# Transposed scores a tick later, head tiles loaded four ticks ahead, a second buffer for the MLP's hidden units, and eight slots of second-layer weights

## The reference

```python
def _L0_xattn_ref(tgt, memory, Wq, Wk, Wv):
    ...
    probs = jax.nn.softmax(scores, axis=-1)
    ...
    tgt2 = att[0]
    return tgt + tgt2

def _L1_xattn_ref(x, y, ...):
    ...
    attn = jax.nn.softmax(jnp.einsum('bhmd,bhnd->bhmn', q, k) * SCALE, axis=-1)
    ...
    x = x + o @ Wproj + bproj
    h = layer_norm(x, gm, bm)
    h = jax.nn.gelu(h @ W1 + b1, approximate=False)
    x = x + h @ W2 + b2
    return x
```

## Time and profile before

| | before |
|---|---|
| runs, us | 1812.53, 1810.10, 1816.04; median 1812.53 |
| profiled execution, us | 1814.68, span 1812.9 |
| VectorE, ScalarE, GpSimd busy, us | 1083.6, 1154.6, 938.3 |
| a matmul of 512 columns, ns (pipelined; start to start about 230) | 395 to 404 |
| an exponential of 128 x 512, ns | 600 |
| VectorE's subtraction for a low half, ns | 690 |
| GpSimd's subtraction for a low half, ns | 1290 |
| mean granted clock of TensorE | 0.987 |

### The profile page before, as it was taken

One profiled execution on the slowest core, in us unless ns is written; L12 is line 12 of the kernel. 1 busy time (PEld: TensorE's weight loads), 2 busy tenths in 40 slices (PEclk: granted clock), 3 DMA queues, 4 the chain that ended last, 5 costly groups with the idle time before them and its releaser, 6 DMA issues.

```text
span 1812.9 us, 23964 instructions
## 1 busy us (share of the span) xinstructions
PE 1724.4 (95%) x7488; PEld 1323.2 (73%) x7488; DVE 1083.6 (60%) x1860; ACT 1154.6 (64%) x1935; POOL 938.3 (52%) x802
## 2 busy tenths in 40 slices
PE   6899998998989899999999999999999999999898
PEld 5677776766666677777777777777777777777686
DVE  4566665477777566666665665666666656563322
ACT  3677764587877665766765576667657665874231
POOL 0454556157665464655555554646555545555241
PEclk8999999999999999999999999999999999999999
DMA  6688989675545575686666566756756675677262
GB/s 233 210 297 282 306 281 362 225 223 173 169 129 185 154 201 135 183 234 163 169 199 187 143 161 187 203 139 194 230 154 165 200 189 147 166 211 242 98 205 93
DMA packets 157102, 354.69 MB, mean 196 GB/s; under 512 B 29232, under 2 KB 47792, under 8 KB 156080
## 3 DMA queue, kind: packets, MB, share of 16 engines
q1 hardware_dynamic: 106096, 187.21, 35.5%
q10 hardware_dynamic: 50880, 165.95, 29.3%
HBM read 251.51 MB, written 82.08 MB: 184 GB/s over the span
## 4 chain that ended last, share of the span: by engine, by line
PE 69%; ACT 9%; issue 5%; DMA 5%; DVE 5%; POOL 4%; SPq 2%; ACTq 1%; DVEq 0%; POOLq 0%
PE ps_d L863 46%; PE ps_o L884 11%; PE ps_t L917 6%; PE ps_s L902 5%; DMA q_st<-negmax_t 2%; ACT p_hi L1026 1%; DMA rs<-o_raw 1%; ACT ps_t L1033 1%; ACT ps_d L937 1%; POOL p_lo L1288 1%; ACT ht L998 1%; PE ps_d L793 1%; DVE negmax L1176 1%; SPq L713 1%; DVE stats L1133 1%
## 5 line engine op out<-in xcount | busy, mean ns | idle before, releaser
L1288 POOL TENSOR_TENSOR p_lo<-p_full,p_hi 128x512 fp32r<-128x512 f32 x288 | 371.4, 1290 | 593.3 <-ACT p_full L1033 592.9
L1026 ACT ACTIVATE p_hi<-ps_t 128x512 fp32r<-128x512 f32 x576 | 345.3, 600 | 364.4 <-PE ps_t L917 359.6
L1176 DVE TENSOR_REDUCE negmax<-ps_s 128x1 fp32r<-128x512 f32 x576 | 389.2, 680 | 135.3 <-PE ps_s L902 134.9
L863 PE MATMUL ps_d<-hT,w_r 128*128 128x512 f32 x1536 | 422.1, 395 | 1.4 <-DVE hT L1081 1.3
L863 PE MATMUL ps_d<-w_r,g_s 128*128 128x512 f32 x1536 | 391.3, 394 | 5.5 <-DMA w_r<-w_scratch 5.5
L863 PEld LDWEIGHTS ps_d<-hT,w_r 128*128 128x128 f32 x1536 | 290.1, 190 | 74.0 <-DVE hT L1081 5.4
L863 PEld LDWEIGHTS ps_d<-w_r,g_s 128*128 128x128 f32 x1536 | 290.6, 190 | 71.2 <-issue 7.1
L1189 DVE TENSOR_TENSOR p_lo<-ps_t,p_hi 128x512 fp32r<-128x512 f32 x288 | 198.8, 690 | 232.2 <-ACT ps_t L1033 231.3
L917 PE MATMUL ps_t<-q_st,k_st 97*128 97x512 f32 x576 | 232.9, 404 | 17.3 <-DMA q_st<-negmax_t 12.1
L884 PE MATMUL ps_o<-p_hi,v_s 128*65 128x512 f32 x576 | 232.3, 403 | 12.6 <-POOL p_lo L1288 6.4
L902 PE MATMUL ps_s<-k_st,q_st 96*128 96x512 f32 x576 | 232.1, 403 | 5.3 <-DVE negmax L1176 5.0
(11 more groups left out here) (99 smaller groups left out, 2174.5 us busy)
## 6 DMA issues: line engine op xcount, KB each, us to landing
w_r<-w_scratch ACTq DMA_DIRECT2D x214, 512.0 KB, 4.9
w_r<-w_scratch SPq DMA_DIRECT2D x42, 512.0 KB, 4.7
v_scratch<-v_out SPq DMA_DIRECT2D x36, 520.0 KB, 5.1
k_scratch<-kq_out SPq DMA_DIRECT2D x36, 512.0 KB, 5.2
q_st<-q_scratch SPq DMA_DIRECT2D x144, 128.0 KB, 4.4
k_st<-k_scratch SPq DMA_DIRECT2D x144, 128.0 KB, 4.2
o_ab<-o_raw SPq DMA_DIRECT2D x144, 128.0 KB, 3.8
w_scratch<-piece_out SPq DMA_DIRECT2D x16, 1024.0 KB, 6.2
```

Of the source, the lines that this page charges most:

```text
L863: ins = nc.tensor.matmul(bank(u), lhs[a], rhs[b], start=(i == 0 and m == 0), stop=(i == 3 and m == 2))
L1026: act.activation(p_hi[:, c], ps_t[:, c % 2], ACT.Exp, scale=SCALE)
L1176: dve.tensor_reduce(negmax[:, h % 2, c:c + 1], ps_s[:, c % 2], AX.X, ALU.max, negate=True).then_inc(s_maxed, 1)
L1288: pool.tensor_tensor(p_lo[:, c], p_full[:, (by_gpsimd(s) - 1) % 2], p_hi[:, c].bitcast(F32), ALU.subtract).then_inc(p_pool_split, 1)
```

## The change

SHIFT goes from 7 to 8 and WEIGH from 9 to 10, STACK_AHEAD from 5 to 4. `h_st` becomes two buffers that lie in the low halves of the two slots of `g_s`: hidden units are emptied there, GELU is applied there in place, and GpSimd overwrites them with the low half. VectorE's wait for the low halves is removed; that a slot is free follows from the order of TensorE's units. The room goes to the second layer's ring, which has eight slots. In the first MLP block (n = 1, ticks of block 2) the turns and the first four hidden units are spread over 13 ticks instead of 9, the first burst is four ticks later, and two hidden units of the next group stand in front of its tick, where there was nothing.

```diff
--- before.py
+++ after.py
@@ -45,10 +45,10 @@
 
 
 
-SHIFT = 7
-WEIGH = 9
+SHIFT = 8
+WEIGH = 10
 POOL_CHUNKS = (0, 2)
-STACK_AHEAD = 5
+STACK_AHEAD = 4
 PRE = 6
 
 COST = {"a": 2.0, "tg": 2.0, "ht": 2.0}
@@ -204,9 +204,9 @@
             else:
                 spread(range(at + 15, at + 22), outs)
                 spread(range(at + 22, at + 35), queries[-6:])
-                spread(range(at + 35, at + 44), turns + hidden(new, 0))
-                burst(at + 44, new, 0, [])
-                spread(range(at + 45, at + 55), hidden(new, 1))
+                spread(range(at + 35, at + 48), turns + hidden(new, 0))
+                burst(at + 48, new, 0, hidden(new, 1)[:2])
+                spread(range(at + 49, at + 55), hidden(new, 1)[2:])
             burst(at + 55, new, 1, second(new, 0)[:2])
             spread(range(at + 56, at + CH + 5), second(new, 0)[2:] + hidden(new, 2))
 
@@ -375,7 +375,7 @@
 
 
 
-W1_RING, W2_RING = 4, 6
+W1_RING, W2_RING = 4, 8
 W1_PIECES = [(n, c) for n in range(1, NP) for c in range(HC)]
 
 
@@ -484,7 +484,7 @@
     g_at = place[0]
     g_s = sb("g_s", [P, 2, 2, 4, T], F32R)
     h_at = place[0]
-    h_st = sb("h_st", [P, 4, T], F32)
+    h_st = [sb(f"h_st_{i}", [P, 4, T], F32, at=g_at + 4 * (2 * i + 1) * 4 * T) for i in range(2)]
     w2_at = place[0]
     w2_r = sb("w2_r", [P, W2_RING, 2, D], F32R)
     w1_at = place[0]
@@ -610,6 +610,9 @@
         if i < PIECES // 2:
             return w1_raw[:, i % 2].rearrange("p c (k j) -> p c k j", k=FC)
         return w2_raw[:, i % 2]
+
+    def hidden_of(n, group):
+        return h_st[GELU_NO[n, group] % 2][:]
 
     def source(kind, i):
         if kind == "h":
@@ -1014,7 +1017,7 @@
             for n, group in PLAN.bursts.get(tick, []):
                 done = GELU_NO[n, group]
                 act.wait_ge(evacuated, ready("hid", n, 4 * group + 3))
-                act.activation(h_st[:], h_st[:], ACT.Gelu).then_inc(gelu_done, 4)
+                act.activation(hidden_of(n, group), hidden_of(n, group), ACT.Gelu).then_inc(gelu_done, 4)
             s = PLAN.t_at.get(tick)
             if s is not None:
                 c = s % TC
@@ -1039,9 +1042,9 @@
                 done = GELU_NO[n, group]
                 if (n, group) in PLAN.by_chunk.get(tick, []):
                     act.wait_ge(evacuated, ready("hid", n, 4 * group + c))
-                    act.activation(h_st[:, c], h_st[:, c], ACT.Gelu).then_inc(gelu_done, 1)
+                    act.activation(hidden_of(n, group)[:, c], hidden_of(n, group)[:, c], ACT.Gelu).then_inc(gelu_done, 1)
                 act.wait_ge(gelu_done, 4 * done + c + 1)
-                act.activation(g_s[:, done % 2, 0, c], h_st[:, c], ACT.Identity).then_inc(g_hi, 1)
+                act.activation(g_s[:, done % 2, 0, c], hidden_of(n, group)[:, c], ACT.Identity).then_inc(g_hi, 1)
             late = tick >= SHARED_FROM
             for u in STORES.get(tick, []) if late else ():
                 store(act, *u)
@@ -1106,11 +1109,8 @@
                 dve.wait_ge(unit_ready, NO[u] + 1)
                 dve.tensor_tensor(xres[n % 2][:, c], bank(u), xres[n % 2][:, c], ALU.add).then_inc(evacuated, 1)
             elif kind == "hid":
-                done = GELU_NO[n, c // 4]
-                if done:
-                    dve.wait_ge(g_lo, 4 * done - 3 + c % 4)
                 dve.wait_ge(unit_ready, NO[u] + 1)
-                dve.tensor_scalar(h_st[:, c % 4], bank(u), col_s[:, 6 * FC + c:6 * FC + c + 1], None,
+                dve.tensor_scalar(hidden_of(n, c // 4)[:, c % 4], bank(u), col_s[:, 6 * FC + c:6 * FC + c + 1], None,
                                   ALU.add).then_inc(evacuated, 1)
             else:
                 if c < TC:
@@ -1293,7 +1293,7 @@
             for n, group, c in G_HALVES.get(tick, []):
                 done = GELU_NO[n, group]
                 pool.wait_ge(g_hi, 4 * done + c + 1)
-                pool.tensor_tensor(g_s[:, done % 2, 1, c], h_st[:, c], g_s[:, done % 2, 0, c].bitcast(F32),
+                pool.tensor_tensor(g_s[:, done % 2, 1, c], hidden_of(n, group)[:, c], g_s[:, done % 2, 0, c].bitcast(F32),
                                    ALU.subtract).then_inc(g_lo, 1)
             for name, c in WHOLE_LO.get(tick, []):
                 whole_low(name, c)
```

## The result

| | before | after |
|---|---|---|
| median of 4 runs, us | 1813.13 (1810.10 to 1816.04) | 1861.35 (1854.28 to 1868.67) |
| ratio | 1 | 1.0266, 95% interval 1.0223 to 1.031 |
| profiled execution, its span | 1814.7, 1812.9 | 1868.67, 1866.8 |
| mean granted clock of TensorE | 0.987 | 0.978 |

The changed kernel is 2.7% slower, 48 us. The forecast was 12 us faster. The interval of the ratio is 8 us wide on either side, and every price that is taken from after's median carries that much.

What follows compares the result with a forecast made beforehand. It took TensorE, working in fixed order and busy 1724.4 of 1812.9 us, as the bound. Terms -16.5 - 8.5 - 8.9 + 3.8 + 17 + 1 = -12.1 us, from the median 1812.5 to 1801; range 1785 to 1820.

Steps and rivals of the forecast that it cites:

- A: Transposed scores one tick later: TensorE's waits for the row of negated maxima and their lowered clock go, -16.5 us.
- rival 3: Removed waits reappear as waits for ScalarE, VectorE and GpSimd, above all in the attention stretch; 1811 us, chance 0.13.
- B: First MLP block's burst: two hidden units fill TensorE's 5.08 us idle during GELU, -8.5 us.
- C: Eight slots of second-layer weights instead of six: both groups of load waits at the end go, -8.9 us.
- D: Last scores: the last transposed tile comes behind 48 hidden-unit matmuls, delaying the last weighting and low halves, +3.8 us.
- E: Head tiles loaded four ticks ahead, behind the row on SyncE: some land late and TensorE waits, +17 us.
- Rival 2: Slower: head tiles issued behind the row set TensorE's pace and drop its clock; 1832 us, chance 0.17.
- F: First MLP block's output projection stays put while its input, the joined heads, comes a tick later, +1 us.
- The slower one: Rival 2: late head tiles set TensorE's pace, one head late in each of 24 groups; 1832 us, chance 0.17.
- rival 1: Head tiles land in time everywhere, since the later issues fall into a gap of loads; 1785 us, chance 0.2.

Runs made afterwards that it cites:

- e6: e2 with the second-layer weight ring back from eight slots to six; 1808.35 us, ratio to before 0.9979.
- e2: After without the shift and the later head tiles (SHIFT 7, WEIGH 9, STACK_AHEAD 5), so the MLP edits alone; 1797.33 us, ratio to before 0.9923.
- e5: After with the MLP's filler one tick later and STACK_AHEAD back to 5; 1792.79 us, ratio to before 0.9896.
- e3: After with STACK_AHEAD back to 5, so head tiles load a tick earlier; 1826.90 us, ratio to before 1.0088.
- e11: After with the filler one tick later and head tiles issued ahead of the row, STACK_AHEAD still 4; 1790.56 us, ratio to before 0.9881.
- e4: After with the MLP's filler one tick later, the block's end left where it is; 1836.54 us, ratio to before 1.0144.
- e7: e2 with STACK_AHEAD 4, so head tiles load a tick later without the shift; 1823.33 us, ratio to before 1.0072.
- e8: After with head tiles issued before the row on SyncE from block 1 on, STACK_AHEAD still 4; 1823.01 us, ratio to before 1.0062.

## Why the prediction was wrong, step by step

The prices by the medians, each step from the run before it: burst -3.8 (before to e6), ring -11.0 (to e2), shift with nothing in its way -4.5 (to e5), filler left behind +34.1 (to e3), loads behind the row +34.5 (to after). Steps of one walk add up by themselves, so their sum of +49.3 is no check of them (48.2 was measured; the medians of before differ by 1.0). In the other order of the last two steps the loads cost 43.7 and the filler 24.8.

The start times of the score tiles in the traces tell where: us, one execution each; the time up to block 1 varies by some 4 us between them and is left out.

| stretch | before | e6 | e2 | e5 | e11 |
|---|---|---|---|---|---|
| block 1 (attention beside the queries) | 144.9 | 144.7 | 144.6 | 140.9 | 139.3 |
| second half of block 2 (first burst) | 83.2 | 76.9 | 77.0 | 76.8 | 76.0 |
| block 3 to the last score | 986.9 | 986.4 | 981.7 | 980.3 | 983.4 |
| last score to the end | 175.1 | 175.4 | 167.2 | 170.0 | 169.9 |

- **A, the transposed scores**, forecast -16.5 with bounds of -6 and -18: mis-sized. Measured -4.5, to -6.8 by way of e11. The row waits went as said (12.1 to none in after; 8.5 in e2 to 3.4 in e5). In the attention stretch the forecast of 5.1 nearly holds (e2 to e5 and e11: 3.7 and 5.3). In the middle it had 7.4. The three executions without the shift take 981.7 to 986.9 us there, with 2.4 to 5.3 us of row waits, the two with it 980.3 and 983.4: a gain of up to 6.6 from before, and next to none from e2. The end is 2.8 us longer with the shift, and what the 4 us of the start are worth can't be read. In part the other engines took the places of the row, which is rival 3's argument. TensorE's waits of 348 to 493, first of before, then of e5:

```profile
PE ps_t L917 <- DMA q_st<-negmax_t: 3.4, 3, 2.2
PE ps_s L902 <- DVE negmax L1176: 2.4, 4, 1.7
...
PE ps_o L884 <- DVE p_lo L1189: 1.3, 3, 0.6
```

```profile
PE ps_o L887 <- DVE p_lo L1189: 4.9, 6, 1.9
PE ps_s L905 <- DVE negmax L1176: 3.5, 5, 1.2
...
PE ps_t L920 <- DMA q_st<-negmax_t: 0.6, 1, 0.6
```

The row gave 2.8 us back, GpSimd's low halves another 1.6, and VectorE took 4.7; but e5 also gets ten matmuls more done in the same 145 us (568 against 558), with a granted clock of 0.99 there, against 0.96.

- **B, the burst**, forecast -8.5: right in mechanism, somewhat less in size. The 5.08 us of the earlier trace rows are gone; in after the GELU runs under two hidden units and the matmuls behind them:

```profile
620.23 5.60 PE L866 MATMUL ps_d<-hT,w_r 128*128 128x512 f32 x24
```

  The stretch with the burst is 6.2 us shorter in e2 and 6.3 in e6. Why the median of e6 fell by 3.8 only is open; its profiled execution has a row wait of 4.1 us in the middle, which e2's hasn't.
- **C, the ring**, forecast -8.9: right. The end is 8.2 us shorter in e2 than in e6, and the medians are 11.0 apart.
- **D, the tail**, forecast +3.8 with bounds of 1 and 6: the mechanism was right, with 1.8 us of idle and a granted clock of 0.79 over 1732 to 1740 behind it; some 2 us by the ends compared above. The timeline of after:

```profile
1732.16 0.45 PE L887 MATMUL ps_o<-p_hi,v_s 128*65 128x512 f32 x1 [0.98 <-DVE p_lo L1189]
...
1733.38 0.92 PE L866 MATMUL ps_d<-w_r,g_s 128*128 128x512 f32 x3 [0.54 <-issue]
```

  Its third gap, 0.28 us at 1734.58, is the wait for a low half.
- **E, the head tiles**, forecast +17, bounds of 0 and 45: the first step that failed. The mechanism was right and the size was not: it measured +34.5, or +43.7 by itself. It took 13 us of waits in the middle and 2 + 2 in the two blocks before. The waits are 19.6 us in 16 times in the middle, and in the two blocks before, from after's waits of 352 to 505 and of 505 to 662:

```profile
PE ps_s L905 <- DMA k_st<-k_scratch: 8.6, 5, 3.5
```

```profile
PE ps_s L905 <- DMA k_st<-k_scratch: 5.0, 3, 3.6
```

  So the middle was short by a third, and the 2 + 2, given without a row of their own, are 13.6. There, but for the one that opens block 1, TensorE was ready for the late heads 9.7 to 12.2 us after the last score of the head two before, for which the working allowed 11.3 at the mean. In the middle the form of the working was right (row, three issues, landing), and its 19 tight heads at 0.9 us, together 17, are close to the 16 at 1.2 that were measured. The step that missed is the discount from 17 to 13, "past part of the weights": most loads did land faster, the last ones of the late heads didn't (6.5 us in the median). And the sum took the waits at their length, with nothing for the clock behind them, which its bound of 45 had. Rival 2 had this mechanism with that clock, E at 45 + 4 against 43.7 measured, though its waits were not these: it has 24 of 1.5 us in the middle, and there were 16 of 1.2 there and 9 more before it. The rule that a DMA takes some 2.0 us and its bytes over the bandwidth (the Trainium skill, DMA: Bandwidth & Descriptors, Anatomy of one DMA) would have made E nothing. That section gives it for transfers that GpSimd issues, and SyncE issues these. The fastest landing, 1.9 us, is near it; the 5.0 to 7.9 us of the late heads decide against it as a rule for loads beside others.
- **F, the join**, forecast +1: right. The projection of the first MLP block waits 1.0 us for it.
- **What was not in the sum**: filler that stays while the weighting, and with it VectorE's inversion, moves. The sum put it at nothing without a reason. This is the second step that failed, 34.1 us by itself and 24.8 beside late loads (D and F are part of it). F asked the right question, what stays while its neighbour moves a tick, for one stage, the join, and not for the rest of what hangs on WEIGH. A list of VectorE's work by tick, before and after, would have shown the inversion enter the ticks of the turned tiles.
- **The rivals.** The slower one came true in mechanism, and its time of 1832 is near e4 (1836.5), where E is alone; partly by luck, since it keeps A at 16.5. Either cost alone leaves the range of 1785 to 1820 (1826.9 with the late filler, 1836.5 with the late loads), so it missed by E's size already, and with both together by 41 us.
- **Slips in the working** that decide nothing: in D, 0.4 + 1.2 + 0.7 - 0.9 is 1.4 and not 1.3, and rival 1 takes 15 off for an E of 17, which would give 1783.

Not tried: SHIFT 8 with a single h_st. By the tables VectorE's hidden unit of the last block would wait for low halves whose input comes after the last transposed tile, which TensorE takes behind those hidden units; if so, the buffers in g_s are what makes the shift possible, but no run shows it. Still open: why late loads cost 17.7 us more with the shift (e4 less e5) than without it (e7 less e2), and why the two errors together cost less than one by one.

## What to carry to other kernels

When a stage is delayed by a tick, list for every engine and queue what moves with it and what stays, and look at each place where the two now meet: here 68.6 us came from two such meetings, and moving the rest along turned 2.7% slower into 1.2% faster. On a queue that issues in order, put first the transfer whose reader comes soonest, and count the issuing time of what stands ahead of it (2.2 us here) against its margin. A removed wait is worth no more than the next-latest engine leaves of it, and one that comes a few times in one execution may be shorter in the next: 12.1 us of row waits in before's profile, 8.5 in e2's, were worth 4.5 by the medians.

## What the runs showed of the hardware

SyncE needs about 0.55 us to issue one DMA, so 2.2 us for the four of a row; four of them ahead of a load cost more than the fastest landing (1.9 us). e8 shows what hangs on it: the same transfers in another order, 38 us.

VectorE's copy of 128x512 (line 1155) has no one duration. Its lines in before, then in after: min, median and max in ns.

```profile
L1155 DVE COPY rs_t<-rinv x36: 418/770/1812, 137.8 to 1681.1; 128x512 f32<-128x512 f32 x36
```

```profile
L1155 DVE COPY rs_t<-rinv x36: 415/427/1809, 140.4 to 1743.0; 128x512 f32<-128x512 f32 x36
```

In before it is 0.42 us where GpSimd does nothing. Where an operation of GpSimd is under way, it takes what is left of that operation and 0.28 us more: at 916.86 GpSimd had 1.24 us to go, and the copy took 1.52. That sum holds within 0.01 us for all 30 of the 36 copies of before that start beside one. This is what made the collision of after so dear: at all six waits for hT the copy starts 0.01 to 0.04 us after an operation of GpSimd and waits it out.

The Trainium skill, SBUF — State Buffer, section SBUF: two separate sides, says that VectorE and GpSimd share a port pair that only one can hold and that the loser blocks, and it says for which operations: those of VectorE in a mode with two ports, as a copy in fp32 within SBUF (the on-chip memory of the tiles), and those with two inputs in SBUF, against an operation of GpSimd that reads SBUF. The trace agrees: the copy is of that kind. VectorE's reductions of scores (0.63 to 0.69 us over all of after) and its subtractions for p_lo (0.65 to 0.69) have at most one input in SBUF, the other lies in PSUM, where TensorE writes, and show no such stretch.
